# Coupling phase: where in the pipeline the final factors alpha and beta are turned

## The reference, cut to what matters

```python
def _twist(x):
    o_r, o_i, p_r, p_i = jnp.split(x, 4, axis=-1)
    return jnp.concatenate([p_r, -p_i, -o_r, o_i], axis=-1)
...
out = x
for _ in range(NUM_CYCLES):          # 3
    tf = _coupling_net(out, ...)     # 512 -> 512 -> 256 -> 128 -> 1, gelu, sigmoid at the end
    combined = 0.7 * gf + 0.3 * tf   # gf: the same kind of net on the mean over tokens
    coupling = BASE_COUPLING + adaptive_range * (combined - 0.5) * 2.0
    out = out + coupling * _twist(out)
return out                           # then layernorm(x + out)
```

## Time and profile before

| what | us |
|---|---|
| median of 3 runs | 2389.9 |
| lowest and highest run | 2387.33, 2393.57 |
| span of the profiled execution, from the first to the last instruction | 2389.4 |
| start of the coupling phase's first transposes in it | 1782.15 |

### The profile page before, as it was taken

The page is one execution under the profiler, slowest core; times in us unless marked ns, Lnnn a source line. Parts: engine busy times, 40 slices in busy tenths (PEclk is TensorE's granted clock), DMA queues, the critical chain, the costliest instruction groups (busy, mean ns, idle before and its releaser), DMA issues. The chain is left out here.

```text
span 2389.4 us, 31918 instructions
## 1 busy us (share of the span) xinstructions
PE 1988.3 (83%) x10328; PEld 1433.3 (60%) x10328; DVE 1687.0 (71%) x3039; ACT 1043.8 (44%) x1788; POOL 1029.5 (43%) x879
## 2 busy tenths in 40 slices
PE   4579989899898998989985899999948888878772
PEld 4455655656556566556533788888736666666651
DVE  5468878788788887888773666667654777776765
ACT  1145545354453545535452222222214555555653
POOL 2567668576675766758720222222201212221121
PEclk9689999999999999999997999999979999898986
DMA  4000010100101000010004011211030121122111
GB/s 129 0 27 1 14 41 1 54 1 19 37 1 54 1 23 32 1 36 1 32 5 154 36 69 64 79 53 53 18 110 36 53 71 38 32 70 70 53 36 53
DMA packets 54719, 99.25 MB, mean 42 GB/s; under 512 B 5040, under 2 KB 8112, under 8 KB 54576
## 3 DMA queue, kind: packets, MB, share of 16 engines
q1 hardware_dynamic: 54576, 97.38, 11.9%
HBM read 63.82 MB, written 33.55 MB: 41 GB/s over the span
## 5 line engine op out<-in xcount | busy, mean ns | idle before, releaser
L588 ACT ACTIVATE a_probs<-a_exp 128x512 f32<-128x512 f32 x512 | 285.1, 596 | 353.6 <-PE a_exp L701 350.2
L437 DVE TENSOR_REDUCE a_neg_max<-a_max 128x1 f32<-128x512 f32 x512 | 341.1, 684 | 91.3 <-PE a_max L686 86.0
L293 POOL TENSOR_TENSOR a_rstd<-a_rstd,a_minus_half 128x16 f32<-128x16 f32 x64 | 186.3, 2911 | 189.3 <-DVE a_rstd L422 189.3
L686 PE MATMUL a_max<-a_stack 96*128 96x512 f32 x512 | 229.9, 451 | 34.2 <-DVE a_neg_max L437 34.0
L1405 POOL TENSOR_TENSOR f_mixed<-f_tw,f_beta 128x512 f32<-128x512 f32 x64 | 96.1, 1520 | 346.0 <-DVE f_beta L1504 170.1
L686 PEld LDWEIGHTS a_max<-a_stack 96*128 96x128 f32 x512 | 97.3, 191 | 173.3 <-DVE a_neg_max L437 119.7
L574 ACT ACTIVATE a_stack<-a_exp 96x512 fp32r<-96x512 f32 x256 | 138.4, 589 | 141.4 <-PE a_exp L673 140.6
L658 PE MATMUL a_t<-a_w_hi,a_zT_hi 128*128 128x384 f32 x512 | 175.8, 343 | 29.1 <-DVE a_v L405 29.1
L701 PE MATMUL a_exp<-a_stack 100*128 100x512 f32 x512 | 185.3, 404 | 2.9 <-ACT a_stack L578 2.0
L955 POOL TENSOR_TENSOR r_part<-r_part 128x512 f32<-128x512 f32 x32 | 45.8, 1431 | 313.8 <-DVE r_part L1002 313.8
L673 PE MATMUL a_exp<-a_ident,a_n 128*96 128x128 f32 x1024 | 143.1, 284 | 43.4 <-ACT a_stack L574 35.0
(11 more groups left out here) (239 smaller groups left out, 5299.4 us busy)
## 6 DMA issues: line engine op xcount, KB each, us to landing
a_z<-x SPq DMA_DIRECT2D x8, 1024.0 KB, 5.6
a_y<-x SPq DMA_DIRECT2D x32, 256.0 KB, 2.7
x<-a_y SPq DMA_DIRECT2D x32, 256.0 KB, 2.0
r_xn<-x SPq DMA_DIRECT2D x8, 1024.0 KB, 5.7
r_cn<-ctx SPq DMA_DIRECT2D x8, 1024.0 KB, 7.8
x<-r_xn SPq DMA_DIRECT2D x8, 1024.0 KB, 4.3
f_xn<-x SPq DMA_DIRECT2D x8, 1024.0 KB, 5.7
x<-f_xn SPq DMA_DIRECT2D x8, 1024.0 KB, 7.2
```

What stands on the lines that cost most here:

```text
L293: nc.gpsimd.tensor_tensor(rstd[:, c], rstd[:, c], minus_half[:, :], ALU.pow).then_inc(pool_step, 1)
L437: nc.vector.tensor_reduce(neg_max[:, t, ROW + h:ROW + h + 1], bank_max[i % 2][:, :], AX_X, ALU.max, negate=True).then_inc(max_done, 1)
L588: nc.scalar.activation(probs[:, kt % 2, h, :], bank_exp[i % 2][:, :], ACT.Exp, scale=float(1.0 / np.sqrt(np.float32(HD)))).then_inc(exp_do ...
L686: mm(bank_max[i % 2][:, :], stack[0:ROW, par, h, t * P:(t + 1) * P], stack[0:ROW, par, HG + h, :], start=True, stop=True).then_inc(score_d ...
```

## The change

The stage `("scale", "run", 0)` leaves the end of the list. The stage `("scale", "old", 0)` comes in behind `("turned", "new", 2)`, so in the following pass, where the entry that was `run` is `old`. On PE the eight small transposes now come behind all sixteen input transposes and ahead of `l3` of cycle 0. On DVE the three operations now come behind the reduction and low half of tile 2 and ahead of those of tile 3. Nothing else changes: the same instructions are issued, each engine in the new order.

```diff
 STAGES = [
     ("transpose", "new", 0), ("transpose", "new", 1), ("transpose", "new", 2), ("turned", "new", 0),
-    ("transpose", "new", 3), ("turned", "new", 1), ("turned", "new", 2), ("l3", "run", 0), ("turned", "new", 3),
+    ("transpose", "new", 3), ("turned", "new", 1), ("turned", "new", 2), ("scale", "old", 0), ("l3", "run", 0), ("turned", "new", 3),
     ("first", "new", 0), ("l3_out", "run", 0), ("z", "run", 0), ("y", "old", 0), ("first_out", "new", 0),
...
-    ("normalise", "next", 0), ("couple", "run", 2), ("l2_out", "new", 0), ("gate", "new", 2),
-    ("scale", "run", 0)]
+    ("normalise", "next", 0), ("couple", "run", 2), ("l2_out", "new", 0), ("gate", "new", 2)]
```

## The result

| | median us | lowest to highest | runs |
|---|---|---|---|
| before | 2390.57 | 2387.33 to 2395.41 | 20 |
| after | 2397.22 | 2392.20 to 2400.46 | 20 |

The ratio after to before is 1.0021, with a 95% interval from 1.0015 to 1.0028. The change makes the kernel slower by 0.15 to 0.28% by the interval, 3.6 to 6.7 us; the two medians lie 6.65 us apart. 2382.5 had been forecast, with a range of 2377 to 2389: the time lies outside it, on the other side of no change. That is 3.0 us more than the 2389.4 of before, so the two traces compared here hold less than half of the 6.65 us.

The account below looks back on a forecast made before the run. No engine is full; a chain between engines sets each pass, with DVE setting the time behind the boundary. 5.3 - 0.6 - 0.6 + 3.3 = 7.4 us off gave a median of 2382.5, range 2377 to 2389.

Parts of the forecast that it names:

- DVE's waits: Ahead of DVE's first reduction at six boundaries: the wait goes when transposes precede the turning, 5.3 us off.
- The readings behind tile 2: DVE's three readings of the turned factors, moved behind tile 2: a pause of 0.1 us each, 0.6 us lost.
- Rival 5: At the boundaries, PE's whole 3.7 us wait would come off: 20 us, to 2370; chance under 0.01.
- three signs: Wrong if PE is last at `first`, clock is 0.5 over `l3`, or three or more passes have slow cycle 1.
- the turning moves behind tile 3 and ahead of `l3`: PE's order at six boundaries: slow clock there costs 0.6 us, within bounds of 0 to 4.2.
- The bound of 4.2 us: Six boundaries losing 0.7 us each if tile 3, turning and `l3` all run at 1.2 GHz.
- Rival 4: PE still at 1.2 GHz when `first` begins, 21.6 us lost against 4.7 gained: 2406.8; chance 0.04.
- Rivals 2 and 4: Slow clock through tile 3, turning and `l3`: 2389.4, chance 0.12; slow clock reaching `first`: 2406.8, chance 0.04.
- The fourth term: Inside the passes: two of three slow cycles 1 vanish as passes get shorter, 3.3 us off; the least certain term.
- The collision of the loads: A later entry's load, leaving SP earlier, may delay the reload of x: counted 0, at worst 3 us in all.

Follow-up runs that it names:

- e1: Changed kernel plus 22 extra matmuls that compute nothing, on PE between tile 2's transposes and the wait for tile 3: 2384.45 us, 0.9979 of before.
- e3: Changed kernel with the turning one place earlier, between tile 2's and tile 3's transposes, no extra work: 2383.75 us, 0.9975 of before.
- e6: Changed kernel plus 11 extra matmuls that compute nothing, on PE between tile 2's transposes and the wait for tile 3: 2390.70 us, 0.9999 of before.
- e2: Kernel before plus 16 extra matmuls that compute nothing, on PE between the last gate product and the turning: 2385.27 us, 0.9979 of before.
- e7: Kernel before plus 12 extra matmuls that compute nothing, in PE's gap ahead of cycle 1's layer 2: 2388.37 us, 0.9993 of before.
- e11: Kernel with the turning ahead of tile 3's transposes, with `l3` of cycle 0 also moved ahead of them: 2403.09 us, 1.0050 of before.

## Why the prediction was wrong

**What held.** DVE, not PE, is the engine that bounds the boundary when PE is fast; `first` at 10.4 us behind the gate's end (e1 and e3: 10.2 to 10.45 from the second boundary on). DVE's waits fell from 7.3 to 2.0 us. The readings behind tile 2 cost what was taken: from 1961.05, the start of tile 2's low half, to 1962.06 are 1.01 us instead of the usual 0.60, so 0.41, which is 0.13 above the step's own 0.28 (0.04 to 0.19 over the six boundaries). Rival 5 was rightly excluded. Of the three signs that it had named for being wrong, two stood in the trace: PE and not DVE was last at `first`, and the clock was 0.50 over `l3`.

**The step that failed** is "the turning moves behind tile 3 and ahead of `l3`". I took 0.6 us out of bounds of 0 to 4.2. The first sum shows it: 64.60 against the 59.8 that DVE alone allows (e3), so 4.8 us were lost, the whole upper bound and a little more. The reason given was that a part of the slow stretch would fall into the idle time. A part did: the clock fell at about 1957.9, 1.6 us ahead of tile 3. It was no help, because the clock then stayed at 0.50 all the way to `first`.

The reading behind it was wrong too. I argued from the fast `l3` of the earlier trace rows that the slow stretch is over by then. But that was one boundary. In the next one tile 3, behind the twelve slow transposes, still took 1.09 us, the slow pace, and PE came to `first` with 0.45 us to spare instead of 1.47:

```profile
2035.02 0.50 PE L1675 MATMUL f_w<-f_xT_hi,f_w_hi 128*128 128x512 f32 x1 [0.45 <-DVE f_xT_lo L1418]
```

And in the kernel before twelve transposes stood between the gap and that `l3`, and in the boundary shown they were the ones that ran at 0.50, at a place where only DVE's wait of 0.85 us hung on them. The change moved just these ahead of the gap. So PE comes out of its gap 6.5 us behind the gate's end instead of 3.7, with tile 3, the turning and `l3` still to do before `first`. At 0.50 these take 4.73 us, which ends at 11.2; DVE is ready at 10.4. e1 shows that the clock is the cause: with PE kept busy in the gap the loss is gone. Whether the slow clock met these three because the transposes had gone, or because the idle time had grown from 3.7 to 5.1 us, no run separates cleanly. e6 speaks for the transposes: it has them ahead of the gap and only 3.2 us of idleness left, less than the 3.7 of before, and from the second boundary on tile 3 to `first` ran at 0.54 to 0.69.

The bound of 4.2 us was also added up wrongly. Its own terms, 1961.0 + 1.09 + 0.96 + 3.1, give 1966.15 and not 1965.6, a loss of 1.2 us a boundary and not 0.7. That 0.8 was measured is nearer to 0.7 by luck: `l3` took 2.7 us at 0.50 and not 3.1.

The rule that the prediction quoted from the Trainium skill, "TensorE: Matmul & The Clock Gate", section "HAM oscillation — how this bites in real kernels", on waits that recur in every tile, was the better guide than the row set against it. The trace of the changed kernel agrees with it, at 0.50 or 0.51 from tile 3 to `first` six times in six.

**Rival 4, given 0.04,** came true in part. `first` was slow in all six boundaries, by 0.14 to 1.40 us, 4.8 together, 28% of its price for twelve slow matmuls in each. Rivals 2 and 4 are one mechanism at two depths and should have shared one chance, much larger than 0.16.

**The fourth term,** 3.3 us for fewer slow cycles 1, came to 1.4 (sum 3). Of the six stretches of sum 3 the first and the third lost their slow cycle 1 and took 2.1 and 1.6 us less, but the last got one and took 1.6 more. That the sign was right is luck: the reason given was a pass 0.8 us shorter, and the boundaries became longer. e1, e2 and e3 had 2.8 to 3.2, with the same boundary work in different places, so a shorter or quieter boundary does change which passes meet a slow cycle 1. How it chooses is not settled here: e7 tried to remove the cause on its own place and stayed unclear.

In numbers: 7.4 us off were forecast. In place of 5.3 - 0.6 - 0.6 + 3.3 stand 5.3 - 0.6 - 4.8 - 4.8 + 1.4 = 3.5 us more. With the 0.8 us saved ahead of these stretches and 0.3 lost behind them, that is the 3.0 us of the spans.

The collision of the loads did not show: the reload of x took 9.4 us to landing before and after, and e1 and e3 load about as early as the changed kernel (tile 3 starts 6.5 and 6.9 us behind the gate's end, against 6.5) and have no loss.

The version to keep is e3: the same instructions as before, the turning between tile 2's and tile 3's transposes. It is at 0.9975 of before (0.9966 to 0.9984), and faster than the changed kernel by more than that. Why its `first` was nearly always fast, behind a `l3` at 0.50 as in the changed kernel, was not tested.

## What to carry to other kernels

When work is moved ahead of a wait, ask what it did behind the wait: on TensorE it may have been the work on which the slow clock fell. Price the moved wait as its length and everything that PE does between its end and the next thing that another engine waits for, at the half rate, until a trace shows otherwise. And look for a place in the middle of the idle time before one at either end of it.

## What the runs showed of the hardware

The granted clock of an idle stretch need not tell what follows. It was 1.00 over 3.70 us of idleness and 1.00 over 2.49 us in e11, and in both the fall came in the work behind, to 0.50 for the transposes and to a mean of 0.61 for `first`. In the changed kernel it came earlier, within the idle time itself: 1.00 over its first 3.50 us and 0.51 over the last 1.58.

Matmuls that compute nothing made a kernel faster by 0.4% (e1 against the changed kernel, 0.9979 against 1.0021 of before) and by 0.2% (e2 against before). In e11 2.49 us of idleness directly ahead of `first` went with 4.42 us for its twelve matmuls instead of 2.90. In e3 about as much idleness ahead of tile 3, 3.5 us earlier, went with 3.34 (2.56 us of it, second boundary), and in four of the six boundaries with 2.90. In the kernel before 1.47 us directly ahead of `first` went with 2.90.
